# One attention and feed-forward layer on 8 cores: PSUM evacuations of the weight fold moved from VectorE to ScalarE, and two steps of the second norm stage put in another order on ScalarE

## The reference

```python
# block 1
y = layernorm(x)                                   # over the 2048 columns, eps 1e-5
n = y * rsqrt(mean(y*y) + 1e-6) * norm_query_w
q = (n @ W_in.T).reshape(.., 16, 128) @ W_q.T
k = patterns @ W_k.T;  v = patterns @ W_v.T        # 16 heads x 1024 patterns x 128
p = softmax(sigmoid(beta) * q @ k.T)               # per head, 1024 wide
a = (p @ v).reshape(.., 2048)
x = x + (a * rsqrt(mean(a*a) + 1e-6) * norm_retrieved_w + y)
# block 2
z = layernorm(x)
g = silu((z @ w_gate) * s_gate) * ((z @ w_up) * s_up)   # 8192 wide, int8 weights
x = x + (g @ w_down) * s_down
```

## Time and profile before

| | |
|---|---|
| median of the 2 runs shown | 2321.06 us (2208.31 and 2433.81) |
| the profiled execution | 2196.68 us |
| its span, slowest core (7) | 2195.1 us |
| the other cores' spans | from 2167.1 us |
| PE, ACT, DVE, GpSimd busy | 82%, 27%, 11%, 8% of the span |
| fold stage | about 9 to 144 us |
| q, k/v and attention | about 144 to 625 us |
| second norm stage | about 625 to 774 us |
| gate/up and down stage | about 774 to 2195 us |

### The profile page before, as it was taken

The page is one execution under the profiler, slowest core; times in us unless marked ns, Lnnn a source line. Parts: engine busy times, 40 slices in busy tenths (PEclk is TensorE's granted clock), DMA queues, the critical chain, the costliest instruction groups (busy, mean ns, idle before and its releaser), DMA issues.

```text
span 2195.1 us, 20633 instructions; the slowest of 8 cores (2167.1 to 2195.1 us)
## 1 busy us (share of the span) xinstructions
PE 1805.7 (82%) x8489; PEld 839.8 (38%) x8489; DVE 245.4 (11%) x472; ACT 602.6 (27%) x573; POOL 175.3 (8%) x239
## 2 busy tenths in 40 slices
PE   2249958888831189999999999999997979979795
PEld 2224434343311034444444444444443434434342
DVE  3530000000035600000000000000000020010102
ACT  1251165555555311111111111111113222212220
POOL 2200030000001200000000000000000010010101
PEclk9659958888865589999999999999998989989898
DMA  8600040000033122222222222222222121121301
GB/s 253 211 1 0 1 153 1 0 1 1 1 131 118 77 77 77 77 77 77 77 77 77 77 77 77 77 77 77 77 77 91 39 91 49 56 89 39 101 24 58
DMA packets 42370, 154.67 MB, mean 70 GB/s; under 512 B 6181, under 2 KB 6182, under 8 KB 36902
## 3 DMA queue, kind: packets, MB, share of 16 engines
q0 software_dynamic: 23984, 84.00, 11.3%
q1 hardware_dynamic: 18294, 69.35, 9.8%
HBM read 103.10 MB, written 16.78 MB: 55 GB/s over the span
## 4 chain that ended last, share of the span: by engine, by line
PE 76%; DVE 6%; ACT 6%; DMA 5%; issue 4%; POOL 2%; SPq 0%; DVEq 0%; ACTq 0%; POOLq 0%
PE PS L958 20%; PE PS L973 20%; PE PS L1098 19%; PE PS L486 5%; PE PS L580 3%; PE PS L595 2%; DMA out<-arena 2%; ACT arena L624 2%; DMA arena<-patT 1%; PE PS L644 1%; PE PS L617 1%; PE PS L611 1%; DVE arena L332 1%; POOL arena L815 1%; DVE arena L790 1%
## 5 line engine op out<-in xcount | busy, mean ns | idle before, releaser
L1098 PE MATMUL PS<-arena 128*128 128x512 bf16 x1956 | 449.0, 384 | 48.7 <-DVE arena L1037 38.8
L958 PE MATMUL PS<-arena 128*128 128x512 bf16 x2048 | 455.1, 381 | 5.4 <-DMA arena<-wu 5.4
L973 PE MATMUL PS<-arena 128*128 128x512 bf16 x1984 | 438.7, 379 | 0.0
L1098 PEld LDWEIGHTS PS<-arena 128*128 128x128 bf16 x1956 | 192.8, 99 | 289.8 <-issue 65.7
L958 PEld LDWEIGHTS PS<-arena 128*128 128x128 bf16 x2048 | 201.1, 98 | 248.7 <-issue 9.0
L973 PEld LDWEIGHTS PS<-arena 128*128 128x128 bf16 x1984 | 193.9, 98 | 234.3
L982 ACT ACTIVATE arena<-PS,sgc_s 128x1024 bf16<-128x1024 f32 x64 | 71.3, 1113 | 735.6 <-PE PS L967 735.6
L1065 ACT ACTIVATE arena<-arena 128x2048 bf16<-128x2048 int8 x64 | 121.7, 1908 | 342.7 <-PE PS L1087 333.7
L624 ACT ACTIVATE arena<-PS 128x1024 bf16<-128x1024 f32 x128 | 129.2, 1024 | 66.9 <-PE PS L611 66.9
L990 DVE TENSOR_TENSOR arena<-arena 128x1024 bf16<-128x1024 bf16 x64 | 44.3, 692 | 851.2 <-ACT arena L985 851.2
L486 PE MATMUL PS<-arena 128*128 128x512 bf16 x496 | 117.9, 392 | 8.2 <-ACT arena L463 8.2
(11 more groups left out here) (109 smaller groups left out, 955.4 us busy)
## 6 DMA issues: line engine op xcount, KB each, us to landing
arena<-wg POOLq DMA_DIRECT2D x64, 512.0 KB, 3.5
arena<-wu POOLq DMA_DIRECT2D x64, 512.0 KB, 4.2
arena<-win SPq DMA_DIRECT2D x16, 1024.0 KB, 7.2
arena<-x SPq DMA_DIRECT2D x16, 1024.0 KB, 5.5
arena<-wd SPq DMA_DIRECT2D x64, 256.0 KB, 2.6
arena<-patT SPq DMA_DIRECT2D x16, 512.0 KB, 4.0
x1sp<-arena SPq DMA_DIRECT2D x8, 1024.0 KB, 3.9
arena<-x1sp POOLq DMA_DIRECT2D x32, 256.0 KB, 5.0
```

Source lines behind the costliest of these rows:

```text
L958: En.matmul(PG[:, half * 512:half * 512 + 512], wgb[:, hc * 128:(hc + 1) * 128], x1nT3[:, hc, half * 512:half * 512 + 512], start=(hc == 0 ...
L973: En.matmul(PU2[:, half * 512:half * 512 + 512], wub[:, hc * 128:(hc + 1) * 128], x1nT3[:, hc, half * 512:half * 512 + 512], start=(hc == ...
L1098: En.matmul(PS[:, j * 512:(j + 1) * 512], fuse3[:, ic, j * 128:(j + 1) * 128], wdb[:, c * 512:(c + 1) * 512], start=(ic == 0), stop=(ic == ...
```

## The change

Three edits.

- **Fold evacuation.** The 32 evacuations of L332 (128 x 8 x 128, float32 in PSUM to bf16) are done by ACT (`activation` with Copy) where DVE did them (`tensor_copy`). The matmuls that reuse the PSUM region wait for ACT's counter where they waited for DVE's.
- **Scale and bias of the first norm.** The statistics chain gets one more small step, minus the mean. The two steps after the square roots become plain products of two columns where they were products of three factors. Their number stays three.
- **Order in the second norm stage.** `G_sqrt(k-1)` is called right behind `G_V2(k-1)`, ahead of `G_SQ(k-2)`; `G_xar(k)` is called behind `G_SQ(k-2)` and `G_T1(k-2)`. The order of the calls on DVE, GpSimd, PE and SyncE stays as it was.

```diff
             for hf in range(2):
                 if h >= 1:
-                    wait(Rt, cV, fold_evac_val[h - 1][hf])
+                    wait(Rt, cS, fold_evac_val[h - 1][hf])
...
-                wait(Rv, cT, t1)
-                t2 = cV.tick()
-                Rv(lambda En, d=dst3, s=src3, hf=hf:
-                   En.tensor_copy(d[:, hf * 8:hf * 8 + 8, :],
-                                  s[:, hf * 8:hf * 8 + 8, :]).then_inc(cV.h, 1))
+                wait(Rs, cT, t1)
+                t2 = cS.tick()
+                Rs(lambda En, d=dst3, s=src3, hf=hf:
+                   En.activation(d[:, hf * 8:hf * 8 + 8, :],
+                                 s[:, hf * 8:hf * 8 + 8, :], AF.Copy).then_inc(cS.h, 1))
...
                 lambda En, W=W: En.reciprocal(wrk[:, W + 8:W + 9], wrk[:, W + 6:W + 7]),
+                lambda En, W=W: En.tensor_scalar(wrk[:, W + 13:W + 14], wrk[:, W + 3:W + 4],
+                                                 -1.0, None, ALU.mult),
                 final=cV)
...
-                lambda En, W=W: En.scalar_tensor_tensor(wrk[:, W + 11:W + 12],
-                                                        wrk[:, W + 10:W + 11], -1.0,
-                                                        wrk[:, W + 3:W + 4],
-                                                        ALU.mult, ALU.mult),
...
+                lambda En, W=W: En.tensor_mul(wrk[:, W + 11:W + 12], wrk[:, W + 10:W + 11],
+                                              wrk[:, W + 13:W + 14]),
+                lambda En, j=j, W=W: En.tensor_mul(bbs[:, j:j + 1], wrk[:, W + 9:W + 10],
+                                                   wrk[:, W + 13:W + 14]),
...
         for k in range(NT + 2):
-            if k < NT:
-                G_xar(k)
             if 0 <= k - 1 < NT:
                 G_V2(k - 1)
+                G_sqrt(k - 1)
             if 0 <= k - 2 < NT:
                 G_BN(k - 2)
                 G_SQ(k - 2)
                 G_T1(k - 2)
             if k < NT:
+                G_xar(k)
                 G_P1(k)
                 G_P1s(k)
                 G_S1(k)
...
             if 0 <= k - 1 < NT:
-                G_sqrt(k - 1)
                 G_T3(k - 1)
```

More of the change, by code:

```diff
@@ L384, in B_V1b @@
             chain2_val[j] = VC(
-                lambda En, W=W: En.scalar_tensor_tensor(wrk[:, W + 11:W + 12],
-                                                        wrk[:, W + 10:W + 11], -1.0,
-                                                        wrk[:, W + 3:W + 4],
-                                                        ALU.mult, ALU.mult),
-                lambda En, j=j, W=W: En.scalar_tensor_tensor(bbs[:, j:j + 1],
-                                                             wrk[:, W + 9:W + 10], -1.0,
-                                                             wrk[:, W + 3:W + 4],
-                                                             ALU.mult, ALU.mult),
+                lambda En, W=W: En.tensor_mul(wrk[:, W + 11:W + 12], wrk[:, W + 10:W + 11],
+                                              wrk[:, W + 13:W + 14]),
+                lambda En, j=j, W=W: En.tensor_mul(bbs[:, j:j + 1], wrk[:, W + 9:W + 10],
+                                                   wrk[:, W + 13:W + 14]),
                 lambda En, j=j, W=W: En.tensor_scalar(a1s[:, j:j + 1], wrk[:, W + 9:W + 10],
```

## The result

| | before | after |
|---|---|---|
| median of the runs, us | 2207.37 (10 runs, 2193.49 to 2503.53) | 2145.53 (11 runs, 2129.34 to 2298.8) |
| the profiled execution, us | 2196.68 | 2136.89 |
| its span, slowest core (7 in both) | 2195.1 | 2135.4 |

The ratio of after to before is 0.9705, 95% interval 0.9673 to 0.9738: about 65 us less. Some executions of either kernel ran disturbed, with some cores slower at a lower granted clock; the ratio leaves them out, which is why it is the number to go by and not the two medians. Forecast were 2133 us and faster; 0.9705 of 2196.68 is 2131.9.

The account below looks back on a forecast made before the run. In the fold and second norm stages no engine is full; a chain passing between engines sets their length. Gains of 33.9 and 30 us, 64 off 2196.7, give 2133 us; own range 2124 to 2150, 8 in 10 2105 to 2190.

Parts of the forecast that it names:

- Fold stage: Fold stage, 12 to 145 us before: turns fall from 15.1 to 10.8 us, gain 33.9 us, bounds 22 to 38.
- The tie with the loads: Fold stage: loads of 3.15 MB need 10.9 us per turn against 10.6 for the chain; 10.8 taken.
- The sign that the prediction named for this rival: Fold stage: GpSimd's L303 waiting for the W_in load mid-stage would show that loads had taken over.
- The evacuations: Fold stage: ACT copies take 1.03 us; third starts 2.3 us behind the first, the fourth ends at 4.2.
- The small products: First norm's scale and bias, fold stage: plain products for three-factor ones change 0, within 0.1 us per turn.
- the second term: Fold stage evacuations on ACT: 4.2 us from the first one's start to the fourth's end, at the low clock.
- Second norm stage: Second norm stage: turns fall from 16.3 to 12.4 us; gain 30.7, of which 30 kept, bounds 25 to 34.
- The second loop: Second norm stage: loop through DVE and GpSimd's addition, 11.8 us, 0.6 us under the 12.4 through ACT.
- Loads: Rival, fold stage: loads take over, turns 12.5 us, gain there 22, time 2145 us; chance 0.10.
- One stage gives nothing: Rival: either the fold or the second norm stage gains nothing, time 2165 us; chance 0.09.
- The clock in the down stage: Rival, down stage: a lower granted TensorE clock takes the gain back, time 2245 us; chance 0.05.
- Tables: Example within a rival of chance 0.09: ACT's roots and copies reload tables each turn, 2 x 1.28 us.

Follow-up runs that it names:

- the kernel without the hold: The kernel after with the two small products' second factor given as a 128x1 scalar operand, not a second tensor; ratio 0.9672 (0.963 to 0.9714).
- e8_both_split: Kernel after with scalar-operand small products, statistics of tile k-2 first, addition divided 1408 columns DVE, 640 GpSimd; 2123.94 us, 0.9651 of before.

## Why the prediction was right

**Fold stage: 33.9 forecast, 36.3 measured on core 7.** The mechanism held step by step: 5.16 us from pass to first evacuation, statistics under the evacuations, the root behind the fourth. The start came out at 27.57 (forecast 28.4), the eighth pass at 101.68 (104.0), the turn at 10.59 (10.8). Over the eight cores the mean gain was 34.2. The near hit is in part luck: of three mis-sized terms two were too large and one, put at nothing, was too small.

- *The tie with the loads.* The step "With the DMA engines full, core 3 got 289 GB/s at a share of 0.97", by which a turn could not be under 10.9 and I took 10.8, was wrong: on the same core in the kernel after, full engines moved 311 to 317 GB/s over 20 us each, some 10 us a turn, and without the loads the stage is as long. One window is a lower bound of what a resource can do, not its capacity. The sign that the prediction named for this rival was seen all the same: on core 7 GpSimd's L303 waited for its W_in load ahead of 10 of 16 casts, 33.9 us in all, one of them in the turn above (1.19 us). It was a poor sign, since PE waited for a cast only twice, at the very start (ahead of 13.56 and 20.42); what the load sets is when the cast runs, and so what it comes to lie beside.
- *The evacuations.* "So the third evacuation starts 1.03 + 0.15 + 1.1 = 2.3 us behind the first", at the low clock, gave 4.2 us to the root behind the fourth. In turns at the low clock that is right (4.11, 74.73 to 78.84); where the second head's matmuls ran at the upper clock it was 3.7 (63.02 to 66.73). The bound given for that case, 10.2 us a turn, is what the kernel without the hold shows on core 7 (10.1 to 10.5). The rule of the Trainium skill on the clock that was weighed there ("TensorE: Matmul & The Clock Gate", The HAM clock gate: it falls when PE pauses and returns under load) was worth taking: by it turns tend to 10.2. The trace agrees in part, with 0.50 and 0.98 inside one turn, and 0.50 throughout in the next.
- *The small products*, taken at 0 with 0.1 us to either side. For the change from three factors to two that is right. For the step as a whole it was not: the faster turn brings GpSimd's cast beside it, and single turns lose up to 1.6 us (1.78 where 0.16 stood). The mean over the stage is some 0.35 us a turn (10.59 less the 10.24 of the kernel with the scalar operand, core 7), and it hid part of the gain of the second term. In the trace of before this showed once on core 7, at the start, beside a cast that ended at 31.94. I had not read it:

```profile
30.05 1.89 POOL L303 CAST arena<-arena 128x2048 bf16<-128x2048 f32 x1 [2.51 <-DMA arena<-win]
30.99 0.96 DVE L385 SCALAR_TENSOR_TENSOR wrk_s<-wrk_s 128x1 f32<-128x1 f32 x1 [1.78 <-ACT wrk_s L377]
```

The rule of the Trainium skill that spoke against ACT ("ScalarE: Activation LUTs", Rules for kernel authors), that VectorE is the faster one for simple work, was rightly set aside: ACT's evacuations of float32 from PSUM are 0.93 us apart, DVE's were 1.21.

**Second norm stage: 30 forecast, 29.5 measured on core 7.** The first statistics started at 605.04, 6.0 us behind L788's start (forecast 6.05), and the next ones followed by 12.4 to 12.7 us (forecast 12.4). The first squaring ended about 1 us later behind the barrier than before, since ACT waited 10.5 us for the first load of x where it had waited 9.4; the mean gain over the cores was 30.2. DVE's L788 has no wait, and L766 waits for ACT's squaring, as written. The steps that ran later than they had to are cheap: L709's place behind L870 cost no x load. The second loop was put at 11.8; it is 12.1, so its cover was 0.3 us where I had counted 0.6. That it holds two instructions which exclude each other was not in my sum, only in the rows it was read from.

**Sum.** 64 forecast, 65.8 in the two stages on core 7, 59.7 in its span, 65 over all runs. That the span of core 7 came so near is luck in part: between the stages it got 8.1 us shorter and in the down stage 14.6 us longer, and neither was forecast. The rivals fell as follows. Loads: refuted by the kernel without them. One stage gives nothing: refuted by the two halves alone. The clock in the down stage: mean granted 0.92, PE busy 455.67 us against 455.48 before; refuted. Tables: no turn holds a table load; each of the two stages has one, ahead of its first root (on core 7 at 23.5 and 596.8). The 8.1 us between the stages are nearly all attention, 302.2 us before at a mean granted clock of 0.82 and 295.2 after at 0.84. They go with a clock that differs between cores as much as between the kernels: before, core 0 needed 279.8 us at 0.88.

**The down stage of core 7, +14.6 us, stays open in its cause.** Waits of the kernel after from 1594 us on, core 7 (engine, line, what was waited for: us in total, times, longest):

```profile
DVE arena L1029 <- DMA out<-arena: 49.1, 24, 4.5
PE PS L1095 <- DVE arena L1034: 47.8, 18, 3.8
ACT arena L1062 <- DMA arena<-wd: 12.5, 2, 10.7
```

Before, the same three were 34.9, 38.8 and 9.0 us: DVE waits longer for its stores, and PE for DVE. Cores 6 and 7 have it (540.8 and 541.3 us), the other six of the same execution do not (527.5 to 529.6). In another execution of the kernel after it is cores 0 and 1 (548.2 and 547.5, the others 524.3 to 530.4). Two cores of that one:

```profile
core 0 of [0, 1, 2, 3, 4, 5, 6, 7], span 2141.8 us
DVE arena L1029 <- DMA out<-arena: 55.4, 19, 5.0
PE PS L1095 <- DVE arena L1034: 49.7, 18, 5.6
...
core 2 of [0, 1, 2, 3, 4, 5, 6, 7], span 2113.3 us
PE PS L1095 <- DVE arena L1034: 38.3, 18, 3.6
DVE arena L1029 <- DMA out<-arena: 36.6, 23, 2.7
```

Core 1 ended within 0.1 us of core 0 and shows the same waits. Over 14 executions of the kernel after there are 56 such pairs of neighbours (0 and 1, 2 and 3, and so on). In 5 of them the two spans differ by at most 1.5 us, and their mean spans are 2135 to 2144; the other 51 have a median of 2120. The executions that hold such a pair took 2137 to 2146 us, the others 2126 to 2137. Equal spans alone are not the sign: in the kernel before, two pairs ended 0.5 and 0.8 us apart at 2193 and 2190, against a median of 2189. The start of the stage is a better one. In all 13 traces there are 52 pairs, and in three the cores entered the down stage within 0.8 us of each other, each counted from its own first instruction: the two above and cores 2 and 3 of the kernel without loads. These six cores needed 540 to 548 us, all others 522 to 537.

This is a correlation, found behind the fact. The counts do not show that the two cores were at the same place at the same moment, since each starts from its own first instruction. That stores of neighbours collide is a guess; a run that sets one core back by a few us would test it and was not made. Nor is it shown whether the change makes such pairs more likely: none of the traced pairs of the kernel before, or of the kernels with half of the change, entered the stage so close.

**The fastest version** is `e8_both_split`: 0.9651 (0.9633 to 0.9669), beside 0.9688 (0.9658 to 0.9719) for the kernel after on the same chip. The intervals overlap, so from the times alone the 0.4% is likely and not shown, the more as one of the control's executions holds a slow pair. In the traces of the two it is seen on every core: the fold stage ends at 103.4 to 105.6 us (106.4 to 108.3 in the control) and the second norm turn is 11.67 us (12.4).

## What to carry to other kernels

Where no engine is full, draw the loop that sets the turn through all engines, move steps off it, and work out the second loop as well: the gain ends there (here 12.4 us with the next loop at 12.1). Before a step is given a price of its own, look at what comes to lie beside it in the new schedule, above all DVE steps with two SBUF tensors beside GpSimd; for a column of 128 values a scalar operand does the same and is not held. The bandwidth in one window is what was asked for, and a bound only if a run without the loads is faster.

## What the runs showed of the hardware beyond this

- The hold between DVE and GpSimd works in both directions, and a tiny operand does not escape it: a product of 128x1 waited 1.6 us for a cast, and a GpSimd addition 0.8 us for one of DVE's. DVE's copy out of PSUM (L898), which has no SBUF input, lasted 1.22 us in all eight tiles, though six of the eight ran wholly beside the same GpSimd addition (core 7 of the kernel after).
- In three of 52 traced pairs both neighbouring cores needed 540 to 548 us for the down stage, where all others needed 522 to 537, as told above, cause open.
- DMA engines at a share of 0.97 moved 289 GB/s in a window of 15 us of the kernel before, and at 0.99 they moved 311 and 317 in windows of 20 us of the kernel after, on core 3 in both.
